# A new steady order for a two-layer cross-attention kernel on TensorE: the two halves of o next to each other, pv split around q, and the context blocks asked for earlier

## The reference

```python
q = jnp.einsum('bte,ef->btf', emb, Wq) + bq
k = jnp.einsum('bml,le->bme', latent, Wk) + bk
v = jnp.einsum('bml,le->bme', latent, Wv) + bv
w = jnp.einsum('bte,bme->btm', q, k) * scale
w = jax.nn.softmax(w, axis=1)
pred = jnp.einsum('btm,bme->bte', w, v)
x = pred + emb
mu, var = jnp.mean(x, -1, keepdims=True), jnp.var(x, -1, keepdims=True)
return (x - mu) * jax.lax.rsqrt(var + EPS) * gamma + beta
```

## Time and profile before

| | |
|---|---|
| median of 3 runs | 1017.89 us (1016.95 to 1019.05) |
| the profiled execution: its own time | 1016.79 us |
| its span, first to last instruction | 1014.9 us |
| PE busy in the span | 989.6 us (98%) |
| DVE, ACT, POOL busy | 876.8, 664.1, 567.6 us |
| granted clock of TensorE, mean | 0.995 |

### The profile page before, as it was taken

How to read it: one execution, slowest core, us unless ns; L and a number is a source line. 1 busy time by engine, 2 the same in 40 slices (tenths; PEclk the granted TensorE clock), 3 DMA queues, 4 the chain that set the end, 5 groups by cost and what they waited for, 6 DMA issues and landing times. The chain is left out here.

```text
span 1014.9 us, 23859 instructions
## 1 busy us (share of the span) xinstructions
PE 989.6 (98%) x6940; PEld 930.9 (92%) x6940; DVE 876.8 (86%) x2616; ACT 664.1 (65%) x1864; POOL 567.6 (56%) x522
## 2 busy tenths in 40 slices
PE   7989999999999999999999999999999999999985
PEld 6879999999999999999999999999999999999975
DVE  4788889988988998888988988898898889888867
ACT  2457767666766666776766676677667666667642
POOL 0134575556566555656555556655565665556574
PEclk9999999999999999999999999999999999999998
DMA  8653434544444454443454444345444445544101
GB/s 213 134 113 77 104 80 97 109 99 102 101 98 78 100 113 98 97 99 84 90 108 97 105 99 98 79 97 114 97 97 100 90 87 105 115 96 97 54 19 37
DMA packets 373958, 98.32 MB, mean 97 GB/s; under 512 B 308488, under 2 KB 357786, under 8 KB 373914
## 3 DMA queue, kind: packets, MB, share of 16 engines
q1 hardware_dynamic: 371370, 96.98, 44.2%
q10 hardware_dynamic: 2544, 0.80, 0.4%
HBM read 83.06 MB, written 14.68 MB: 96 GB/s over the span
## 5 line engine op out<-in xcount | busy, mean ns | idle before, releaser
L680 PE MATMUL oq_bank<-probs,raw 125*128 125x224 f32 x1488 | 302.8, 353 | 1.7 <-ACT probs L929 1.7
L680 PEld LDWEIGHTS oq_bank<-probs,raw 125*128 125x128 f32 x1488 | 272.2, 190 | 2.3 <-ACT probs L929 1.2
L913 ACT ACTIVATE probs<-probs,neg_max 125x224 f32<-125x224 f32 x378 | 177.8, 472 | 143.7 <-DVE neg_max L1194 143.6
L1521 POOL TENSOR_TENSOR psum<-probs 125x672 f32<-125x672 f32 x62 | 100.1, 1615 | 243.8 <-ACT probs L929 243.8
L656 PE MATMUL score_bank<-qT_hi,cT_hi 128*125 128x224 f32 x768 | 199.6, 286 | 3.9 <-ACT cT_hi L870 1.8
L657 PE MATMUL score_bank<-qT_hi,cT_lo 128*125 128x224 f32 x768 | 188.9, 273 | 0.0
L929 ACT ACTIVATE probs<-probs,rsum 125x224 f32<-125x224 f32 x378 | 150.8, 471 | 10.8 <-DVE rsum L1210 9.4
L1584 POOL TENSOR_TENSOR y_out<-z,gamma_row 112x512 f32<-112x512 f32 x62 | 93.9, 1536 | 113.9 <-ACT z L953 113.9
L656 PEld LDWEIGHTS score_bank<-qT_hi,cT_hi 128*125 128x125 f32 x768 | 145.2, 189 | 8.8 <-ACT cT_hi L870 3.4
L661 PE MATMUL score_bank<-qT_lo,cT_hi 128*125 128x224 f32 x768 | 147.1, 273 | 0.0
L657 PEld LDWEIGHTS score_bank<-qT_hi,cT_lo 128*125 128x125 f32 x768 | 145.4, 189 | 0.0
(11 more groups left out here) (136 smaller groups left out, 2038.9 us busy)
## 6 DMA issues: line engine op xcount, KB each, us to landing
raw<-in_ctx_dram SPq DMA_DIRECT2D x64, 375.0 KB
cb<-in_ctx_dram SPq DMA_DIRECT2D x248, 92.0 KB
x<-in_x_dram SPq DMA_DIRECT2D x32, 448.0 KB, 3.6
xb<-in_x_dram SPq DMA_DIRECT2D x124, 112.0 KB, 3.0
out_dram<-y_out SPq DMA_DIRECT2D x31, 448.0 KB, 6.7
cb<-in_ctx_dram SPq DMA_DIRECT2D x124, 3.5 KB
y<-in_L_xattn_Wq_dram SPq DMA_DIRECT2D x2, 512.0 KB, 5.5
Wq_next<-in_L_xattn_Wq_dram SPq DMA_DIRECT2D x2, 512.0 KB, 12.6
```

The source lines that it names most:

```text
L680: ins = nc.tensor.matmul(o, raw[0:MP, u.slot, c, cols], probs[0:MP, u.par4, c, :], start=(c == 0), stop=(c == MC - 1))
L913: ins = act.activation(probs[0:MP, u.par4, c, :], probs[0:MP, u.par4, c, :], ACT.Exp, bias=neg_max[0:MP, u.par4, c:c + 1], scale=-1.0, acc ...
```

## The change

PE's turn before, with half numbers: s(a,0), o(b-1,1), z-transposes(b,0), s(a,1), s(a,2), z-transposes(b,1), pv(b-1,0), q(b,0), pv(b-1,1), q(b,1), o(a,0), d(b), s(b,0), s(b,1), o(a,1), s(b,2), q(a+1,0), pv(a,0), d(a+1), pv(a,1), q(a+1,1), o(b,0). There are six stretches of fp32 work in it. After: pv(a-1,1), s(a,0), o(b-1,0), o(b-1,1), z-transposes(b,0), s(a,1), s(a,2), z-transposes(b,1), pv(b-1,0), q(b,0), q(b,1), pv(b-1,1), d(b), s(b,0..2), o(a,0), o(a,1), d(a+1), pv(a,0), q(a+1,0), q(a+1,1). There are four. ACT, DVE and POOL get new orders that go with it, the opening is rewritten in the same sense, and SP asks for the first half of a batch's raw context ahead of x. No instruction is added or removed in the steady turns.

```diff
@@ SP @@
                     load_cb(a(+0))
                 if a(+1).later(1):
                     load_xb(a(+1))
+                if a(+0).later(0):
+                    load_ctx(a(+0), 0)
                 if a(+1).later(1):
                     load_x(a(+1))
                 if a(+0).later(0):
-                    load_ctx(a(+0), 0)
                     load_ctx(a(+0), 1)
                 store(b(-2))
@@ PE @@
             def turn(i, j):
                 a, b = units(i, j)
+                pv_product(a(-1), 1)
                 score_product(a(+0), 0)
+                o_product(b(-1), 0)
                 o_product(b(-1), 1)
                 transpose_x(b(+0), 0)
                 score_product(a(+0), 1)
...
                 q_product(b(+0), 0)
+                q_product(b(+0), 1)
                 pv_product(b(-1), 1)
-                q_product(b(+0), 1)
-                o_product(a(+0), 0)
                 spread_d(b(+0))
                 score_product(b(+0), 0)
                 score_product(b(+0), 1)
+                score_product(b(+0), 2)
+                o_product(a(+0), 0)
                 o_product(a(+0), 1)
-                score_product(b(+0), 2)
+                spread_d(a(+1))
+                pv_product(a(+0), 0)
                 q_product(a(+1), 0)
-                pv_product(a(+0), 0)
-                spread_d(a(+1))
-                pv_product(a(+0), 1)
                 q_product(a(+1), 1)
-                o_product(b(+0), 0)
@@ ACT, first part @@
                 ctxT_hi(a(-1), 2)
-                d_out(a(-1))
                 if j is not None or i > 2:
                     standardise(a(-2), 0)
+                o_hi(b(-2), 0)
+                if j is not None or i > 2:
                     standardise(a(-2), 1)
                 ctxT_hi(a(-1), 3)
                 o_hi(b(-2), 1)
@@ DVE, the part around the moments of a, new order @@
+                score_max(a(+0), 0)
+                moments(a(-1), 0)
                 half_moments(a(-1), 1)
-                moments(a(-1), 0)
                 moments(a(-1), 1)
-                ctxT_lo(a(+0), 1)
-                q_lo(a(+0), 1)
                 add_eps(a(-1))
                 turn_ctx(a(+0), 2)
                 shift(a(-1), 0)
-                o_lo(b(-1), 0)
+                score_max(a(+0), 1)
                 shift(a(-1), 1)
@@ POOL @@
+                sum_probs(b(-1))
+                inverse_deviation(a(-1))
                 scale(b(-2), 1)
                 add_beta(b(-2), 0)
                 add_beta(b(-2), 1)
-                sum_thirds(b(-1))
-                sum_two(b(-1))
-                inverse_deviation(a(-1))
-                sum_probs(b(-1))
                 scale(a(-1), 0)
                 add_beta(a(-1), 0)
-                scale(a(-1), 1)
                 sum_thirds(a(+0))
                 sum_two(a(+0))
+                sum_probs(a(+0))
+                scale(a(-1), 1)
```

150 lines of the change are left out of this document (77 added, 73 removed).

## The result

The changed kernel takes 1020.28 us (median of 11 runs, 1019.81 to 1022.86), the kernel before on the same chip 1018.09 us (11 runs, 1016.88 to 1021.85). The ratio is 1.0023, with a 95% interval of 1.0012 to 1.0034: slower by 0.23%, where I had forecast 0.2% faster. The profiled execution of the changed kernel took 1019.81 us with a span of 1017.9 us, 3.0 more than that of before. The medians differ by 2.2.

What follows compares the result with a forecast made beforehand. It took the steady turns to be bound by what PE issues. Stretches -2.1, z +1.5, opening 0 and end -1.5 summed to -2.1 us: 1014.7 against the profiled 1016.79, so 1015.8 for the median; range 1012 to 1030.

Steps and rivals of the forecast that it cites:

- the steady turns: The thirty repeated turns: 2.1 us saved on fp32 stretches, 1.5 us lost waiting for z.
- the opening: Work ahead of the steady turns: one 0.87 us wait hidden, a new one of 0.7 to 1.0; taken as 0.
- the end: After the last steady turn: z(62) comes earlier with PE's work ahead unchanged, so 1.5 us less (0.7 to 2).
- The stretches: Two of six fp32 stretches on PE go: 0.07 us a turn (0.03 to 0.09), 2.1 us over thirty.
- entries and exits of the vanished stretches: Part of the saving on PE's fp32 switches, taken as 0.035 us a turn.
- z of unit a: ACT's z ready at 6.20 us against PE's 6.19: a wait of 0.05 a turn, 1.5 over thirty.
- rival B: z late by 0.15 to 0.5 us in every turn: 1023 us, within 1018 to 1030; chance 0.22.
- rival D: PE's sequencer waits in the loop go too: up to 3.6 us less, 1012.2 us; chance 0.07.
- rival C: DVE's residual runs into POOL's work, holding PE at pv(b-1,0) for 0.85 us a turn: 1040 us; chance 0.13.
- DMA: Earlier context-block requests and SP's new order cost nothing; without DVE's idle time as cover, 5.7 us at most.

Runs made afterwards that it cites:

- e6: Changed kernel with PE's d(a+1) moved behind pv(a,0) and ACT taking d out later, just ahead of q(a+1,1); one execution, 1026.61 us.
- e10: Changed kernel with ACT's loop body beginning and ending elsewhere, the order of its instructions unchanged; 1020.09 us, ratio 1.0023.
- e13: Kernel before, with PE's loop body beginning at pv(a-1,1) as in the changed kernel, no engine's order changed; 1018.86 us, ratio 0.9998.
- e4: Changed kernel with DVE's first maximum of s(a,0) moved behind the first nmr, to make z earlier; 1034.64 us, ratio 1.0161.
- e11: Changed kernel with SP's order of before, x asked for ahead of both halves of the raw context; 1020.26 us, ratio 1.0023.
- e3: Changed kernel with DVE's subtraction for layer 1's Wv moved from ahead of the steady turns into the first one; 1020.32 us, ratio 1.0029.
- e8: Changed kernel with unit 62's power moved ahead and POOL's betas of 61 and rest of 62 held until unit 65's dot products are done; 1018.81 us, ratio 1.0003.
- e1: Changed kernel with POOL's power of unit 62 moved ahead of the gamma of 61 and a sum of 63; 1018.9 us, ratio 1.0008.
- e2: Changed kernel with POOL's gamma and beta of unit 62 held until both dot products of unit 65 are done; 1021.83 us, ratio 1.0033.
- e9: Changed kernel with unit 62's power moved ahead and the last unit's first two maxima on DVE ahead of unit 63's remaining moments; 1018.77 us, ratio 0.9998.
- e12: Changed kernel with four edits: maximum behind nmr, residual behind o's small part, unit 62's power ahead, last maxima ahead of moments; 1015.07 us, ratio 0.9970.

## Why the prediction was wrong

The forecast was a sum of -0.6 for the steady turns, 0 for the opening and -1.5 for the end, -2.1 us. In the traces they are +0.05, +0.6 and +2.4, together +3.0.

**The steady turns, -2.1 + 1.5.** Their sum of -0.6 came out as +0.05, and each term was off.

The stretches: I took 0.07 a turn for two of them. r to d does take 0.32 and d 0.154, as forecast; the term that fails is the 0.035 for entries and exits of the vanished stretches, for which my rows gave 0 to 0.02. The two exits that went are r to scores, 0.07, and o to scores, which by the earlier trace rows costs nothing, and that nothing I then raised to 0.035. e6 gives 0.06 for a stretch whose exit is behind d, so a stretch is not dear; the one of the two that ended in o was free. That leaves 0.03 to 0.04 a turn, at my lower bound. The first turns of the loop show it: 29.780 to 29.752.

z of unit a: I walked the chain to 6.20 against PE's 6.19 and took 0.05 a turn. In an unrolled turn z's transposes start 6.27 after pv(a-1,1) ends, with PE due at 6.18: 0.09 late. The walk was good to 0.07, but with no spare that makes 0.09 a turn, where I had taken 0.05. What it lacked is the jump of ACT's loop, which lies between nmr and z in the new order as it did in the old one, but where z had 0.65 to 0.9 us to spare before. With it z is 0.28 late in every second turn. 11 x 0.28 and some seven turns of 0.09 are 3.7 us in place of 1.5; by e10 the jump has 1.2 of them and the short walk the other 2.5. That is rival B in part of the turns, at the low end of its price.

PE's jump, rival D: I put the 0.12 a turn that the loop adds to PE's own sequencer and gave its going 0.07. It did go: 0.27 in every second turn became 0.01, 11 x 0.26 = 2.9 us gained. e13 corrects the reading: 0.11 of it, 1.2 us in all, was a wait for DVE behind a residual that POOL held, which the new order does not have. So the level steady turns are the sum of -2.9 (D), about -1.1 (stretches) and about +3.7 (B), with one turn that waited 0.4 for context blocks. I had D and B as exclusive cases with a chance each, and they came together, with nearly equal sizes. That the measured time lies inside B's 1018 to 1030 is luck: D had paid for B.

**The residual and POOL, rival C.** Not in the changed kernel, but nearer than 13 in 100 suggests. I had computed DVE at 8.9 and POOL at 9.1; the trace has DVE ahead by 0.31. e4, meant to help, crossed the line in 28 of its turns, e11 in two. The mechanism was right; the price was 0.58 a turn, where I had 0.85. The Trainium skill, "SBUF — State Buffer", section "SBUF: two separate sides", states that DVE with two SBUF inputs and GpSimd take a shared port pair as an exclusive lock. The traces agree: the residual and the dot product, which have two SBUF inputs, go from 0.75 to 1.6 and more against POOL, and the maximum, which has one in PSUM, stays at 0.38 beside the same POOL operations.

**The opening, 0.** It came out as +0.6. s(b0) does wait 0.87 as forecast, in place of the 0.87 of o(a1,0), but q(a2) waits 0.58 behind the first residual, which I had not seen and which e3 could only move. The mark at the end of the first steady turn lies between 98.3 and 101.0 us in the traces with the new opening, though all of them start s(a1,0) at 54.9 to 55.2. What differs is TensorE's clock: in the seven traces with 98.3 to 98.6 it stands at 1.00 from 59.8 at the latest, in the seven others it is 0.50 for 3.4 us (99.7 and 99.9) or 6.8 us (100.3 to 101.0) between 60 and 68. The windows of the changed kernel and of e8:

```profile
59.10:68.00 8.90, 7.18 (x58) 6.40 (x57) 7.48 (x26) 4.66 (x13) 0.00 (x0) 1.00 0.60 108
```

```profile
61.20:67.90 6.70, 5.82 (x27) 5.80 (x28) 3.91 (x12) 2.86 (x10) 0.00 (x0) 0.50 0.72 110
```

The traces of before and of the changed kernel both have the clock back at 59.1, so these two can be compared: 0.6. Why the clock falls later in some executions stays open.

**The end, -1.5.** This is the step that failed: "this end is nearer by 1.5 us" came out as 2.4 us longer in the trace, and with it the kernel is slower instead of level. e1 brings the ratio from 1.0023 to 1.0008; those two intervals overlap, but of the kernels whose steady turns are nearly the same, the five without the power moved (the changed kernel, e2, e3, e10, e11) lie at 1.0023 to 1.0033 and the three with it (e1, e8, e9) at 0.9998 to 1.0008.

The chain that I walked for z(62), 5.5 to 6.2, was right for every engine but POOL: 5.8 once the power is free. I left POOL's queue out of it. In a steady turn the power waits for the variance and not for the queue. POOL's timeline in one:

```profile
863.66 0.70 POOL L1571 TENSOR_TENSOR rstd<-ve,minus_half 112x2 f32<-112x2 f32 x1 [1.43 <-DVE ve L1275]
```

In the last turn there is no unit 64, so PE has no d (0.15) and no q (2.67) between the two halves of pv(62), and the variance comes some 2.8 us earlier against POOL's work. That is more than the 1.43 that POOL had spare. The last sums of 63 and the gamma of 61, which stand ahead of the power in every turn, now hold it for 1.7 us.

What I had also not costed is what an idle PE brings: the clock falls behind it. In the changed kernel pv(63,0) and q(65) are 1.2 and 0.4 longer for it. The old order is not free of this either, which its one trace hides. Of the 35 executions of before that were run beside e10, e11, e3 and e12, the 20 with a mean granted clock of 0.995 took 1016.2 to 1018.6 us and the 15 with 0.992 to 0.994 took 1018.2 to 1021.0, median 1019.3; all 11 of the changed kernel have 0.992 to 0.994. So roughly half of the 2.2 us between the medians goes with the clock, at the end or in the opening; these are not the executions of the ratio above, for which the clock of before is not on record.

And "PE does the same work ahead of it, so this end is nearer" holds only up to z: e9 has z 1.2 us earlier and gives 1.15 back. With the power moved and no half clock the end is 50.0 to 50.2, no nearer than the 50.0 of before, so no order tried had the 1.5 us. I put that to pv(63,1), which now follows both halves of q and so puts unit 63's moments among the last unit's maxima and scalings; no run moves it back, and this cause is not shown.

**DMA, 0.** Right to within 0.4 us: one turn near the end waited that much in this trace; SP's order made no difference.

The range of 1012 to 1030 holds the 1020.28. The chance of slower, 0.35, was on B and C; the cause that decided, POOL's queue in the last turns with the half clock behind it, was in none of the rivals.
